# Small products of ones in TensorE's pauses, and a first rotation shared by three engines, in a one-core attention and feed-forward kernel

## The reference

```python
q = _proj(Wq, bq, x);  k = _proj(Wk, bk, c);  v = _proj(Wv, bv, c)   # x: layernorm of the item, c: context
q = _rope(q, d_rope);  k = _rope(k, d_rope)                          # x*cos + neg_half*sin on half the channels
scores = jnp.einsum('bhqd,bhkd->bhqk', q, k) / jnp.sqrt(jnp.float32(kc))
p_attn = jax.nn.softmax(scores, axis=-1)
out = _proj(Wo, bo, jnp.einsum('bhqk,bhkd->bhqd', p_attn, v))
x = x + jnp.tanh(g_xattn[0]) * out
# feed-forward: two products with 4-bit weights, silu(gate) * up, one product down, a root-mean-square norm
x = x + jnp.tanh(g_ffn[0]) * _L0_ffn_ref(_layernorm(x, axis=-1), ...)
```

## Time and profile before

| | us |
|---|---|
| median of three runs | 725.92 (725.85 to 726.64) |
| profiled execution | 726.46 |
| its span, first to last instruction | 724.6 |
| PE busy | 692.7 (96%) |
| DVE busy | 610.9 (84%) |
| ACT busy | 521.2 (72%) |
| POOL busy | 476.1 (66%) |

### The profile page before, as it was taken

One profiled execution on the slowest core, in us unless ns is written; L12 is line 12 of the kernel. 1 busy time (PEld: TensorE's weight loads), 2 busy tenths in 40 slices (PEclk: granted clock), 3 DMA queues, 4 the chain that ended last, 5 costly groups with the idle time before them and its releaser, 6 DMA issues.

```text
span 724.6 us, 13389 instructions
## 1 busy us (share of the span) xinstructions
PE 692.7 (96%) x4678; PEld 338.6 (47%) x4678; DVE 610.9 (84%) x825; ACT 521.2 (72%) x925; POOL 476.1 (66%) x403
## 2 busy tenths in 40 slices
PE   3789999999999999999999999999999999999995
PEld 2334434433444344434443444655565556555653
DVE  6698889888988898888889779766899789977894
ACT  1228888888888888888888876665666566666653
POOL 2756655796678667866633129876697669766773
PEclk7659999999999999999999999999999999999998
DMA  7786777687767877877663202000001000100011
GB/s 242 179 207 160 173 197 200 164 186 209 200 167 182 212 191 180 196 200 190 153 160 70 86 24 74 0 1 1 0 1 45 14 1 0 45 16 0 4 42 72
DMA packets 48935, 80.59 MB, mean 111 GB/s; under 512 B 14436, under 2 KB 17892, under 8 KB 48868
## 3 DMA queue, kind: packets, MB, share of 16 engines
q1 hardware_dynamic: 47712, 78.99, 43.0%
q10 hardware_dynamic: 1156, 0.74, 0.4%
HBM read 45.11 MB, written 32.24 MB: 107 GB/s over the span
## 4 chain that ended last, share of the span: by engine, by line
PE 50%; POOL 26%; issue 14%; DVE 4%; DMA 3%; ACT 1%; SPq 1%; POOLq 0%; ACTq 0%; DVEq 0%
PE pv_ps L845 18%; POOL probs L299 15%; PE s_ps L815 14%; POOL probs L303 9%; PE st_ps L827 9%; DVE max_rows L1119 3%; PE st_ps L800 2%; PE st_ps L788 2%; PE st_ps L857 2%; PE st_ps L794 2%; DMA qk_stack<-image 2%; DMA image<-split_head 1%; POOL over_stack L223 1%; DMA inverse_scratch<-sums 1%; PE pv_ps L910 1%
## 5 line engine op out<-in xcount | busy, mean ns | idle before, releaser
L1119 DVE TENSOR_REDUCE max_rows<-s_ps 128x2 f32<-128x1024 f32 x256 | 305.3, 1213 | 42.6 <-PE s_ps L815 41.9
L956 ACT ACTIVATE probs<-st_ps 128x512 f32<-128x512 f32 x512 | 277.5, 595 | 54.0 <-PE st_ps L827 43.7
L318 ACT ACTIVATE probs<-s_ps,gu_sc 128x512 f32<-128x512 f32 x176 | 117.6, 685 | 84.4 <-PE s_ps L404 84.2
L299 POOL TENSOR_TENSOR probs<-probs 128x512 f32<-128x512 f32 x88 | 120.3, 1371 | 69.5 <-ACT probs L318 69.2
L845 PE MATMUL pv_ps<-probs,v_all 128*32 128x256 f32 x2048 | 163.4, 391 | 2.2 <-ACT pv_all L962 2.2
L815 PE MATMUL s_ps<-qk_stack 48*128 48x512 f32 x512 | 132.7, 516 | 7.6 <-DVE max_rows L1119 5.5
L170 DVE SCALAR_TENSOR_TENSOR proj<-s_ps,gu_sc,proj 128x512 f32<-128x512 f32 x132 | 98.8, 749 | 11.1 <-PE s_ps L404 1.9
L827 PE MATMUL st_ps<-qk_stack 50*128 50x512 f32 x512 | 107.9, 411 | 0.0
L420 PE MATMUL st_ps<-dn_head,over_input 128*128 128x512 f32 x264 | 104.8, 423 | 1.0 <-DVE over_input L181 1.0
L815 PEld LDWEIGHTS s_ps<-qk_stack 48*128 48x128 f32 x512 | 49.4, 190 | 114.0 <-issue 70.9
L845 PEld LDWEIGHTS pv_ps<-probs,v_all 128*32 128x32 f32 x2048 | 40.6, 108 | 98.3 <-ACT probs L956 82.3
(11 more groups left out here) (122 smaller groups left out, 891.4 us busy)
## 6 DMA issues: line engine op xcount, KB each, us to landing
qk_stack<-image SPq DMA_DIRECT2D x60, 384.0 KB, 6.2
image<-split_rest SPq DMA_DIRECT2D x32, 256.0 KB
image<-split_head SPq DMA_DIRECT2D x31, 256.0 KB
image<-split_head SPq DMA_DIRECT2D x62, 128.0 KB
xt_all<-x_dram SPq DMA_DIRECT2D x16, 256.0 KB, 3.7
ct<-ctx_dram SPq DMA_DIRECT2D x16, 256.0 KB, 3.5
scale_of<-inverse_scratch SPq DMA_DIRECT2D x16, 256.0 KB
out_dram<-over_stack SPq DMA_DIRECT2D x16, 256.0 KB, 2.0
```

Source lines behind the costliest of these rows:

```text
L299: nc.gpsimd.tensor_tensor(pair[:, n], parts[T_ % 2][:, 2 * n], parts[T_ % 2][:, 2 * n + 1], ALU.add).then_inc(pairs_ok, 1)
L318: nc.scalar.activation(parts[T_ % 2][:, k], gu_ps[(2 * k) % BANKS], ACT.Copy, scale=gu_sc[:, k, T_ % IT:T_ % IT + 1]).then_inc(gate_read, 1)
L956: nc.scalar.activation(probs[at % PROBS][:, tile % 4, :], st_ps[item % ST_BANKS][:], ACT.Exp).then_inc(st_read, 1)
L1119: nc.vector.tensor_reduce(out, s_ps[item % S_BANKS][:], AXIS_X, ALU.max).then_inc(s_read, 1)
```

## The change

**Products of ones.** A product `hold` multiplies 128 by 128 ones with 128 by 192 ones, into a bank that nobody reads. Twenty stand ahead of the projection of item 1, five behind that of item 2, and one behind every score slot of item 0 except slots 3, 5 and 6 (13 in all). For the last thirteen TensorE first waits until ScalarE has read the second projection bank of item 2 (`st_read`).

**First rotation.** The product of half 1 with the cosine goes from VectorE to GpSimd (`first_cosine`), ahead of GpSimd's work on items 1 and 2. Both roundings go from VectorE to ScalarE (`first_head`), ahead of ScalarE's three stores. VectorE does both additions and then both subtractions; before, it finished half 0 and had it stored ahead of half 1.

```diff
+HOLD_LONG, HOLD_SHORT, HOLD_COLS = 20, 5, 192
@@ TensorE, first stage
+                still = v_ones[1].rearrange("p k j q c -> p (k j q c)")
+                def hold(bank):
+                    nc.tensor.matmul(bank[:, 0:HOLD_COLS], still[:, 0:P], still[:, 0:HOLD_COLS], start=True, stop=True)
...
                 project_rot(pe, 0)
                 project_pass(pe, 0)
+                pe.wait_ge(values_set, 2)
                 for n in (1, 2):
+                    for _ in range(HOLD_LONG if n == 1 else 0):
+                        hold(pv_ps)
                     project_rot(pe, n)
                     project_pass(pe, n)
+                for _ in range(HOLD_SHORT):
+                    hold(pv_ps)
+                pe.wait_ge(st_read, ST_NO["rot", 2] + 1)
                 for slot in range(SLOTS):
                     score(pe, 0, slot)
+                    if slot not in (3, 5, 6):
+                        hold(st_ps[ST_NO["rot", 2] % ST_BANKS])
@@ ScalarE, ahead of store_head(act, 0, 1)
+            def first_head(act, w):
+                act.wait_ge(rotated[w], 1)
+                nc.scalar.activation(split_head[:, w], proj[0][:, w], ACT.Copy).then_inc(heads[w], 1)
@@ VectorE, rotate_first
                 nc.vector.tensor_tensor(cross[:, 0], tile[:, 0], sin[:, 0], ALU.mult).then_inc(crossed_first, 1)
+                dve.wait_ge(st_read, ST_NO["pass", 0] + 1)
+                nc.vector.tensor_tensor(cross[:, 1], tile[:, 1], sin[:, 1], ALU.mult).then_inc(crossed, 1)
...
                 dve.wait_ge(cosine_first, 1)
                 dve.wait_ge(crossed, 1)
-                split(dve, nc.vector, 0, 0)
-                nc.vector.tensor_tensor(tile[:, 1], tile[:, 1], cos[:], ALU.mult).then_inc(cosine, 1)
+                nc.vector.tensor_tensor(tile[:, 0], tile[:, 0], cross[:, 1], ALU.add).then_inc(rotated[0], 1)
                 dve.wait_ge(cosine, 1)
-                split(dve, nc.vector, 0, 1)
+                nc.vector.tensor_tensor(tile[:, 1], tile[:, 1], cross[:, 0], ALU.add).then_inc(rotated[1], 1)
+                for w in two:
+                    dve.wait_ge(rotated[w], 1)
+                    dve.wait_ge(heads[w], 1)
+                    nc.vector.tensor_tensor(split_rest[:, w], tile[:, w], split_head[:, w].bitcast(F32), ALU.subtract).then_inc(rests[w], 1)
@@ GpSimd, behind inverse_dev(pool, 0)
+            def first_cosine(pool):
+                pool.wait_ge(crossed, 1)
+                nc.gpsimd.tensor_tensor(proj[0][:, 1], proj[0][:, 1], cos[:], ALU.mult).then_inc(cosine, 1)
```

More of the change, by code:

```diff
@@ L1010, in _ @@
                     if n == 1:
+                        for w in two:
+                            first_head(act, w)
                         store_head(act, 0, 1)
@@ L1102, in rotate_first @@
                 nc.vector.tensor_tensor(cross[:, 0], tile[:, 0], sin[:, 0], ALU.mult).then_inc(crossed_first, 1)
+                dve.wait_ge(st_read, ST_NO["pass", 0] + 1)
+                nc.vector.tensor_tensor(cross[:, 1], tile[:, 1], sin[:, 1], ALU.mult).then_inc(crossed, 1)
                 dve.wait_ge(crossed_first, 1)
                 nc.vector.tensor_tensor(tile[:, 0], tile[:, 0], cos[:], ALU.mult).then_inc(cosine_first, 1)
-                dve.wait_ge(st_read, ST_NO["pass", 0] + 1)
-                nc.vector.tensor_tensor(cross[:, 1], tile[:, 1], sin[:, 1], ALU.mult).then_inc(crossed, 1)
                 dve.wait_ge(cosine_first, 1)
                 dve.wait_ge(crossed, 1)
-                split(dve, nc.vector, 0, 0)
-                nc.vector.tensor_tensor(tile[:, 1], tile[:, 1], cos[:], ALU.mult).then_inc(cosine, 1)
+                nc.vector.tensor_tensor(tile[:, 0], tile[:, 0], cross[:, 1], ALU.add).then_inc(rotated[0], 1)
                 dve.wait_ge(cosine, 1)
-                split(dve, nc.vector, 0, 1)
+                nc.vector.tensor_tensor(tile[:, 1], tile[:, 1], cross[:, 0], ALU.add).then_inc(rotated[1], 1)
+                for w in two:
+                    dve.wait_ge(rotated[w], 1)
[4 more added lines that the diff above has]
+                nc.gpsimd.tensor_tensor(proj[0][:, 1], proj[0][:, 1], cos[:], ALU.mult).then_inc(cosine, 1)
             def maxima(dve, n, slot):
@@ L1260, in _ @@
                 inverse_dev(pool, 0)
+                pool.wait_ge(table_in, TABLES)
+                first_cosine(pool)
                 for n in (1, 2):
                     inverse_dev(pool, n)
-                pool.wait_ge(table_in, TABLES)
                 for n in (1, 2):
```

## The result

| | before | changed |
|---|---|---|
| median of the runs, us | 725.88 (725.82 to 726.64, 4 runs) | 734.70 (733.57 to 735.16, 4 runs) |
| ratio | | 1.0118 [1.0102, 1.0133] |
| profiled execution, its span | 726.46, 724.6 | 734.37, 732.6 |
| PE busy | 692.7 (96%) | 711.4 (97%) |

The changed kernel is 8.8 us slower. The forecast was 4 us faster, 721.9. The products of ones are called holds here; no output reads them, and they only cost time and keep TensorE at work.

The account below looks back on a forecast made before the run. The prediction took VectorE's maxima to bound item 0's scores and TensorE, at 0.50 of its clock, step 0. Rotation 0.3, value projection 1.3 and step 0 2.7 sum to 4.3 us off 726.46: 721.9, range 720.6 to 726.8.

Parts of the forecast that it names:

- The scores of item 0: Item 0's score slots: if the clock stays up, holds fit behind the maxima and the value projection's pause goes, 1.3 us.
- the value projection: After item 0's slot 3: takes 1.0 to 1.1 instead of 2.00 us, so VectorE's pause of 1.36 goes; 1.3 us gained.
- step 0: From item 0's last maximum to slot 4's score of step 0, at the high clock: 2.7 us gained.
- the slots' holds: Item 0's score slots: score 0.43 and hold 0.38 fit in a slot of 1.16 us, behind the maxima.
- rival 1: Item 0's scores: the clock falls and the holds bound, 1.50 a slot against 1.16; 730.7 us, chance 0.15.
- 18 to 21 us: Stretch of the earlier trace, TensorE busy throughout and clock back at 1.00; cited against rival 1.
- about nine cold slots: Rival 1's remark on item 0's scores: about nine slots with holds at the low clock undo the gain.
- The rotation: First rotation: GpSimd's cosine blocks VectorE's addition, yet ScalarE's stores start 0.5 us earlier; first score 0.3 us earlier.
- the forecast's ends of −1.5 and +1.3: First rotation: second head 1.5 us earlier without any blocking, 1.3 later with SP's issues all shifted.
- Item 1's first read: Before step 0's first score: came at 45.98, should land near 44.3; late reads could lose up to 1 us.
- The long holds: Twenty before item 1's projection: hidden behind its wait for VectorE, projection at the high clock; worth nothing by itself, only cover.
- Rival 2: Item 0's scores: the clock falls once and comes back, five cold slots cost 1.7 us; 724.0 us, chance 0.18.

Follow-up runs that it names:

- e5: e3 with 352 instead of 192 columns in the slots' holds, and holds of 192 at slots 5 and 6: 723.57 us, ratio 0.9971.
- e8: The changed kernel with slot holds of 352 columns, and 192 at slots 5 and 6: 736.42 us, ratio 1.0117.
- e11: e9 with the changed kernel's rotation and 17 short holds instead of 12: 724.56 us, ratio 0.9981.
- e3: e1 with 12 short holds instead of 5, filling the pause before the first score: 729.19 us, ratio 1.0044.
- e12: e3 with a hold of 192 columns also behind slots 5 and 6: 727.61 us, ratio 1.0023.
- e6: The kernel before with the first rotation's roundings on ScalarE and VectorE's subtractions after both additions, no holds: 725.56 us, ratio 1.0000.
- e2: The kernel before with the changed kernel's first rotation alone, no holds: 729.32 us, ratio 1.0045.
- e7: e5 with the first rotation's roundings on ScalarE and VectorE's subtractions after both additions, as in e6: 722.58 us, ratio 0.9959.
- e9: e7 with slot holds of 288 columns instead of 352: 722.29 us, ratio 0.9948.
- e1: The changed kernel with the first rotation of before, all holds kept: 729.03 us, ratio 1.0065.
- e4: e3 without the holds behind the score slots: 727.15 us, ratio 1.0020.

## Why the prediction was wrong

**The scores of item 0: the step that failed.** The forecast said "if the clock stays up", and gave that 0.52. Its sum took 1.3 from the value projection and 2.7 from step 0, both at the high clock, and put the slots' holds at nothing, as hidden behind the maxima. The clock did not stay, neither gain came, and thirteen slots at 1.66 instead of 1.16 cost 6.5. The mechanism was rival 1's: the clock falls in the pause before the first score, and the holds, at the low clock, bound. The forecast had one stretch of 2.13 busy in 3 us that had kept the clock, and gave the pause of 2.1 us that it expected no term in its sum. It was 3.9 us, since the short holds ended 0.5 us sooner and the first score came 1.2 us later than forecast. e5 against e8 speaks for the pause as the cause, and e11 for it again, with the changed kernel's rotation and no pause; e3 and e12 show that 192 columns in a slot are not enough even without it. In the earlier trace rows stood the warning that I gave too little weight: 8.99 of 9 us busy at 0.50. The changed kernel was busy for 32.00 of 32 and stayed there. I had set against it 18 to 21 us, where the clock came back, "with full-height products as the holds are". Products of ones in thirteen slots did not bring it back in the 34 us that it was low here; in e8, with larger ones, it took 24 us. And e6, with the same projections and the clock still at 0.50 behind them, shows that the stretch of 18 to 21 us was no safe evidence.

**Rival 1's size.** It said 730.7; the profiled execution was 734.37. The hold with the change to and from it costs 0.94, where I had doubled 0.35. A hold is two records of 192 columns; in a chain of its own it takes 0.34 at full clock, as forecast, but between scores 0.52. With the score at 0.72 (0.80 forecast) the slot is 1.66 for 1.50, 2.1 us over thirteen slots. The first score, 0.9 late instead of 0.3 early, is 1.2. The other slots are 0.4, the feed-forward part 1.0, and step 0 gave back 0.8. These add up to 3.9, for 3.7 between the two times. Its remark that about nine cold slots undo the gain does not follow either: nine of 0.34 are 3.1 of the 4.3, and it would take twelve or thirteen.

**The rotation.** What the instructions do to each other was right. Timeline of the changed kernel, to be laid beside the earlier trace rows:

```profile
9.87 0.69 DVE L1126 TENSOR_TENSOR proj<-proj,cos 128x512 f32<-128x512 f32 x1
10.09 1.59 POOL L1139 TENSOR_TENSOR proj<-proj,cos 128x512 f32<-128x512 f32 x1 [4.59 <-DVE cross L1124]
10.58 1.65 DVE L1129 TENSOR_TENSOR proj<-proj,cross 128x512 f32<-128x512 f32 x1
12.26 1.23 ACT L1018 ACTIVATE split_head<-proj 128x512 fp32r<-128x512 f32 x2 [3.04 <-DVE proj L1129]
```

GpSimd's cosine took 1.59 (forecast 1.8), VectorE's first addition 1.65 (forecast 1.6) instead of 0.69, ending 0.55 after GpSimd's. The Trainium skill's exclusive lock ("SBUF — State Buffer", "Who interferes with whom") holds in this stage as in the earlier trace rows. The chain ran as forecast and ScalarE's stores did begin earlier (13.53 for 14.74). What failed is the silent step behind it, that eight stores issued earlier also land earlier. The last was begun at 15.83, 0.24 before the old one's 16.07, and took 6.85 instead of 5.54. In e2 it was 7.19, in e6 6.75. The landing of the eight hardly follows the issue of the heads: these are issued some 1.5 us earlier in e6 and e7, and the last landing comes at 21.47 and 20.85, against 21.61 before. Why the landing takes up to 1.6 longer where the stores stand closer together stays open. By the first score the rotation cost +0.9 instead of −0.3, inside the forecast's ends of −1.5 and +1.3; by e11 against e9 all of the new rotation against roundings alone is 2.3.

**The rest of the sum, tested with the clock kept.** e7 has the terms. Its first score is 0.65 earlier (25.50; forecast 0.3). VectorE's last maximum of item 0 ends at 45.68 instead of 46.99, so item 0's scores give 0.66 more, half of the 1.3. The pause at the value projection is gone, but thirteen slots of 1.22 are 0.06 each over the maxima and give the rest back; with 288 columns this term is 1.1 (e9 and e11: 19.74 from the first score to the last maximum, before 20.84). From the last maximum to slot 4 of step 0 it is 5.88 instead of 8.48, 2.6 of the 2.7. Together 3.9 by slot 4; the span is 4.1 us shorter than before, for a sum of 4.3; by the medians e7 is 3.0 faster and e9 4.0. Item 1's first read, which I feared late, was not in e7: none of item 1's first scores waits for it, where before the first one's weights waited 0.91. In e9, earlier by a microsecond at that place, they wait 0.45. So the gain is real, at the forecast's size, but the change as made doesn't reach it.

**The long holds.** In the changed kernel's profile they were hidden and at full clock, as forecast: item 1's projection waits for VectorE at 16.73 behind them, and took 0.64 instead of 1.12 a record. Rival 2 (the clock falls once and comes back) is excluded for the changed kernel: it fell once and stayed for 34 us. The Trainium skill's second failure mode ("TensorE: Matmul & The Clock Gate") tells of short idles between groups that make the clock swing; no run here swung from group to group. But "it fell once and stayed", the forecast's reading of the trace of before, is not right: there it fell at 10.8, came back at 21.1 and fell again at 27.9 (0.50, 1.00 and 0.50 again in the earlier trace rows). Short dips are in e1's profiled execution, low from 18.0 to 21.4 behind 2.39 us of idleness, and in e9's, low from 47.4 to 50.8, in a stretch of 1.66 busy in 2 us.

**The chances.** Rival 1 had 0.15, and the range ended 4 us below it. The evidence against that mechanism was two stretches of projections, one busy throughout and one with a pause of 0.80 us; for a pause of 2 us and more before scores, that was too little to go down to 0.15.

## What to carry to other kernels

Filler that is to keep TensorE's clock up should cover the whole pause up to the landing that ends it, with room for a late DMA, and should be priced at the low clock between the real products, not in a chain of its own: if it then outlasts the engine it hides behind, losing the clock can cost more than never having had it (the changed kernel, e8). Try the filler's size on the chip; here 192 columns in a slot lost 1.3 to 3.4 us by the medians (e1, e3, e12), 352 won 2.0 (e5) and 288, with the roundings moved, 4.0 (e9), and nothing in the profile of before told them apart. Of work shared out to shorten a chain that ends in stores, read the landing of the last one, not the issue of the first.

## What the runs showed of the hardware that I had not expected

- A TensorE that is busy throughout can stay at the low clock for long: 0.50 for 32.00 of 32 us (changed kernel), for 20.00 of 20 (e8, where it came back after 24 us with the same slots still running). With the clock up the same slots keep it there (e5, 352 columns in a slot), so the level of such a stretch depends on how it began.
- The same pause or the same work can end either way: 2.39 us of idleness behind the long holds lost the clock in e1 and kept it in e3, e4, e5 and e12; the projections of items 1 and 2 brought it back by 21.1 us in the kernel before and not in e6.
- A product of 192 columns (two records) is 0.34 us in a chain of its own, 0.52 between scores, both at full clock, and 0.94 between scores at the low one; of 352 columns 0.79 and 1.47.
- Runs of one kernel can stand in groups with different mean clocks: 4 us apart in e1 (0.980 to 0.983 and 0.975 to 0.976), and in e8 one of 728.02 (0.993) beside 736.42 to 739.27 (0.977 to 0.982).
- The same eight stores, 1.5 MB to DRAM, land 5.54 (before) to 7.19 us (e2) after the last was begun; the four kernels that issue them closer together and have a row here (changed, e2, e6, e7) all have more than 5.54.
